# One of eight PSUM evictions per group given to VectorE in the edge-expansion stage of a graph layer

## The reference, cut to what matters

```
support = layernorm(x) @ W1
msgs = vals[:, None] * support[cols]            # one row of 256 per edge, 212500 edges
agg  = segment_sum(msgs, rows, num_segments=12500) + support
out  = relu(batchnorm(agg));  out = spmm_plus_eye(rows, cols, vals, out @ W2)
x = x + out
x = x + moe(layernorm(x))                       # 8 experts, top 2, D = 256
```

## Time and profile before

| | |
|---|---|
| median of three runs | 4718.69 us |
| span of the profiled execution | 4733.0 us |
| first stage in it | about 140 to 1235 us |
| busy over the span | TensorE 82%, VectorE 74%, ScalarE 64%, POOL 59% |
| busy in 140 to 1240 us | TensorE 83%, VectorE 82%, ScalarE 85%, POOL 68% |
| granted TensorE clock in 140 to 1240 us | 0.97 of full speed |

### The profile page before, as it was taken

How to read it: one execution, slowest core, us unless ns; L and a number is a source line. 1 busy time by engine, 2 the same in 40 slices (tenths; PEclk the granted TensorE clock), 3 DMA queues, 4 the chain that set the end, 5 groups by cost and what they waited for, 6 DMA issues and landing times.

```text
span 4733.0 us, 85423 instructions
## 1 busy us (share of the span) xinstructions
PE 3862.0 (82%) x26914; PEld 3364.9 (71%) x26914; DVE 3483.6 (74%) x9932; ACT 3025.5 (64%) x6515; POOL 2790.4 (59%) x2961
## 2 busy tenths in 40 slices
PE   1688888888798998855788888888888888888888
PEld 1687877788677777734677777777777777777777
DVE  8888888888688888855666777666777667667666
ACT  3688888888777787743555565555555545555555
POOL 0467676767565665456666666666666656666441
PEclk9999999999899999966899898899988989998999
DMA  8788888888888999663333333333333333333221
GB/s 238 278 304 306 309 309 305 311 305 285 286 297 302 302 317 304 235 194 108 91 103 98 97 104 96 97 101 96 99 100 97 97 96 102 97 98 103 77 76 28
DMA packets 308803, 858.01 MB, mean 181 GB/s; under 512 B 47937, under 2 KB 133018, under 8 KB 305852
## 3 DMA queue, kind: packets, MB, share of 16 engines
q0 software_dynamic: 140032, 442.58, 28.5%
q1 hardware_dynamic: 166148, 396.53, 26.5%
q10 hardware_dynamic: 2172, 13.35, 0.8%
HBM read 545.71 MB, written 306.56 MB: 180 GB/s over the span
## 4 chain that ended last, share of the span: by engine, by line
PE 49%; DVE 20%; ACT 10%; issue 10%; another core or an unknown queue 5%; DMA 4%; POOL 1%; SPq 0%; ACTq 0%; DVEq 0%; POOLq 0%
PE ps L1713 11%; PE ps L1734 8%; PE ps L1456 4%; PE ps L1604 3%; PE ps L886 3%; DMA L<-msgd 3%; PE ps L844 2%; PE ps L855 2%; PE ps L1608 2%; DVE S L1402 2%; PE ps L887 2%; PE ps L1606 2%; PE ps L843 2%; ACT A L951 2%
## 5 line engine op out<-in xcount | busy, mean ns | idle before, releaser
L1532 POOL DMA_INDIRECT G<-h,tabT x1440 | 1421.0, 987 | 941.1 <-issue 372.0
L1813 ACT ACTIVATE ps<-ps,b1T 128x500 f32<-128x500 f32 (+1 forms) x432 | 267.1, 618 | 827.1 <-PE ps L1713 551.9
L951 ACT ACTIVATE A<-ps,A 128x256 f32<-128x256 f32 x1728 | 690.4, 513 | 101.8 <-PE ps L887 98.0
L1002 POOL DMA_INDIRECT msgd<-A,tabT x432 | 542.9, 1257 | 307.5 <-ACT A L951 205.8
L1585 ACT ACTIVATE gH<-G,tabT 128x256 fp32r<-128x256 f32 x960 | 449.2, 499 | 222.1 <-remote 95.5
L1564 DVE SCALAR_TENSOR_TENSOR gL<-G,tabT,gH 128x256 fp32r<-128x256 f32 x960 | 459.1, 478 | 138.9 <-ACT gH L1585 90.9
L886 PE MATMUL ps<-winH,DT 128*128 128x256 f32 x1728 | 474.9, 306 | 67.5 <-issue 40.0
L1980 DVE SCALAR_TENSOR_TENSOR X<-ps,X 125x256 f32<-125x256 f32 x800 | 348.0, 478 | 235.1 <-remote 134.2
L1552 DVE TENSOR_SCALAR s<-iota,tabT 128x125 fp32r<-128x125 f32 x1600 | 518.9, 338 | 0.0
L1606 PE MATMUL ps<-gH,s 128*125 128x256 f32 x1067 | 357.8, 336 | 154.0 <-DVE s L1552 66.1
L887 PE MATMUL ps<-winL,DT 128*128 128x256 f32 x1728 | 437.7, 285 | 0.5 <-issue 0.5
(11 more groups left out here) (339 smaller groups left out, 11143.4 us busy)
## 6 DMA issues: line engine op xcount, KB each, us to landing
L<-msgd SPq DMA_DIRECT2D x400, 520.0 KB, 5.7
A<-sbd SPq DMA_DIRECT2D x54, 861.0 KB
msgd<-A SPq DMA_DIRECT2D x100, 325.0 KB
G<-h,tabT POOLq DMA_INDIRECT x1440
winR<-h SPq DMA_DIRECT2D x108, 128.0 KB
A<-in_x SPq DMA_DIRECT2D x10, 1120.0 KB
h<-A ACTq DMA_DIRECT2D x10, 1120.0 KB
acc<-h SPq DMA_DIRECT2D x10, 1120.0 KB
```

What stands on the lines that cost most here:

```text
L951: e.activation(M[:, n, 0:F], psum[4 + v % 4][:, (n % 2) * F:(n % 2 + 1) * F], ACT.Identity, scale=M[:, n, F + 2:F + 3]).then_inc(evc, 1)
L1002: e.indirect_dma_start(msgd, bass.IndirectOffsetOnAxis(ap=idxI[g % 4][:, t:t + 1], axis=0), msg[g % 3][:, t * 4 * RW:(t + 1) * 4 * RW], No ...
L1532: e.indirect_dma_start(B.G[c % GRL], None, of, bass.IndirectOffsetOnAxis(ap=tab3[:, m, 0:1].bitcast(I32), axis=0)).then_inc(gatl[c % GRL], 16)
```

## The change

Of the eight pairs of a group, number 3 (DVP) is evicted by VectorE with one instruction for both tiles: a tensor_tensor whose first stream is the whole bank in PSUM (128x512) and whose second stream is the two weights, each repeated 256 times. ScalarE evicts the other seven pairs as before. VectorE's eviction of group g stands right behind dve_place(g+1) and waits until pair 8g + 3 is expanded. A counter of its own, evd, tells TensorE, POOL and the verdict that the pair is out.

```diff
+DVP = 3
+def act_evicted(v):
+    return 2 * (v + 1 - (v + 1 + 8 - DVP - 1) // 8)

+        def dve_evict(e, g):
+
+            v = 8 * g + DVP
+            M = msg[g % 3].rearrange("p (t k) -> p t k", k=RW)[:, 2 * DVP:2 * DVP + 2, :]
+            e.wait_ge(recd, 3 * (g + 1))
+            e.wait_ge(exq, v + 1)
+            e.tensor_tensor(M[:, :, 0:F], psum[4 + v % 4][:, :].rearrange("p (n f) -> p n f", n=2),
+                            M[:, :, F + 2:F + 3].broadcast_to([P, 2, F]), ALU.mult).then_inc(evd, 1)

# dve_messages
                 if g + 1 < G2:
                     dve_place(e, own, g + 1)
+                dve_evict(e, g)
                 if g % 2 == 0:

# pe_expand
                 if v >= 4:
-                    e.wait_ge(evc, 2 * (v - 3))
+                    if (v - 4) % 8 == DVP:
+                        e.wait_ge(evd, (v - 4) // 8 + 1)
+                    else:
+                        e.wait_ge(evc, act_evicted(v - 4))

# act_messages, scale
                     v = 8 * g + n // 2
+                    if n // 2 == DVP:
+                        continue

# pool_messages
-                    e.wait_ge(evc, 16 * g + 4 * t + 4)
+                    e.wait_ge(evc, act_evicted(8 * g + 2 * t + 1))
+                    if t == DVP // 2:
+                        e.wait_ge(evd, g + 1)

# dve_verdict
-            e.wait_ge(evc, 16 * G2)
+            e.wait_ge(evc, act_evicted(8 * G2 - 1))
+            e.wait_ge(evd, G2)
```

More of the change, by code:

```diff
@@ L388, in build @@
         nrr, trir, bcd, rhsr, selr, slt, spr, prm = (sem(n) for n in ("nrr", "trir", "bcd", "rhsr", "selr", "slt", "spr", "prm"))
-        recd, dlc, dlt, dtc, bcr, dtd, exq, evc, wsl = (sem(n) for n in ("recd", "dlc", "dlt", "dtc", "bcr", "dtd", "exq", "evc", "wsl"))
+        recd, dlc, dlt, dtc, bcr, dtd, exq, evc, evd, wsl = (sem(n) for n in ("recd", "dlc", "dlt", "dtc", "bcr", "dtd", "exq", "evc", "evd", "wsl"))
         msgz, fillm = sem("msgz"), sem("fillm")
```

## The result

The changed kernel takes 5093.17 us (median of four runs, 5088.2 to 5100.23) against 4716.91 us for the kernel before: 376 us more, a ratio of 1.078 (95% interval 1.0762 to 1.0798). Slower was forecast, but the time lies 23 us above the range and 122 us above the predicted one. The profiled execution has a span of 5089.6 us.

A forecast was written before the change was run, and what follows sets the result against it. VectorE was taken as nearest its limit in the first stage, with the loop closing through it. Holds of 307 us, less 124 of old waits, plus 69 for the clock, gave 252 us on 4719: 4971 us, range 4865 to 5070.

The forecast's parts named there:

- ScalarE's saving is worth nothing: First stage: two evictions fewer a group, 78 us in all, only lengthen ScalarE's waits for TensorE; costed at nothing.
- The eviction at 0.69 us: VectorE's new double eviction, 108 times, takes 0.69 us each, bounds 0.19 and 1.00.
- The hold at full clock, 2.18 us: VectorE waits behind dve_place for TensorE's placing and expansion, 2.18 us; with start and eviction 2.92 us, 105 times, 307 us.
- VectorE's old waits are given back, 124 us: VectorE's waits before L738 and L721, 113.6 and 10.2 us, vanish because it gets there later.
- The net of 183 us: First stage: holds of 307 us less 124 us of old waits, before any clock term.
- TensorE is held at L831 and the select: VectorE's late L709 and L730 make TensorE stand there, about 1.2 us at L831; absorbed by its 5 to 6 us spare.
- The clock, 69 us: First stage: clock falls to 0.775, half speed 45% of the time, adding 1.47 us to that share of 105 holds.
- VectorE's other instructions at their old lengths: First stage: the sum has no term for VectorE's untouched instructions getting longer or shorter.
- nearly every restart: Rival: after nearly every hold TensorE restarts at 1.2 GHz, adding 154 us to 183, 5056 us; chance 0.14.
- the clock's bound: Limits of the first stage's clock term: none or all of the holds at half speed, 0 and 154 us.

The follow-up runs named there:

- e8: Changed kernel with 32 unused matmuls filling TensorE's pause and POOL's split moved behind the first scatter: 201 us over the kernel before, ratio 1.0421.
- b0: The kernel before, unaltered, profiled again on another chip: 4725.04 us, evictions' length 1049.4 us.
- e4: Changed kernel with 32 unused matmuls a group filling TensorE's pause before its wait for dve_place: 256 us over the kernel before, ratio 1.0613.
- e6: Changed kernel with POOL's split moved from ahead of the group's four scatters to behind the first: 240 us over the kernel before, ratio 1.0561.
- e10: Changed kernel with POOL's split behind the first scatter and dve_place's second instruction done three times: 380 us over the kernel before, ratio 1.0906.

## Why the prediction was wrong

The mechanism was right: a hold behind dve_place in every group, ended by pair 3's expansion; and slower was given 0.93. Two steps of the sum failed. The term for the clock was too small, 69 us, and the lengths of VectorE's other instructions were left as they were, without a reason. Together they measure 179 us of evictions' length where the sum had 69. The terms, by the prediction's steps:

- *ScalarE's saving is worth nothing.* Right. Its wait for L906 rose by 76 us, and with pair 1, where the same work is taken from it, the time did not move.
- *The eviction at 0.69 us.* Right: 692 ns.
- *The hold at full clock, 2.18 us.* Nearly: 2.42 us of idle time with the pause filled, against 2.22 in the sum. It also came in the last three groups, 108 times in all.
- *VectorE's old waits are given back, 124 us.* Right but for 8 us: 113.6 and 10.2 us became 7.5 and 0.
- *The net of 183 us.* Shown as a kernel (e8): 183 us of evictions' length (190 against b0), +201 us of time, with full clock and the placing instructions at their old lengths. The exact number is in part luck, as said there.
- *TensorE is held at L831 and the select.* Right: 29.8 us before L847 and 30.5 before L859 (L831 and L843 before), and VectorE hardly waits for TensorE behind the hold (7.5 us before L744).
- *The clock, 69 us.* The first failed step. It took the mean clock of a stretch, 0.775, for the share of holds that start at half speed, 0.45. The stage's mean clock was higher than that, 0.83, and still about (3.61 - 2.42)/1.47 = 0.8 of the hold's clock penalty was paid: the half speed falls upon the matmuls right behind the pause, and those are the ones in the hold. Filling the pause gives back 129 us (e4), or 44 us when the split is moved as well (e8 against e6). Nor could the clock be read off TensorE's busy share in other stages: it is 75% in the changed kernel's stage and in e6's (1089.12 of 1461 us, 991.95 of 1324) at clocks of 0.83 and 0.92, and 76% in e10's at 0.80.
- *VectorE's other instructions at their old lengths.* The second failed step, a term put at nothing. In the new rhythm POOL's split runs beside dve_place, and L768, L772, L775 and L798 grew by some 65 us in all (10, 34, 9 and 12), while L729, L713 and L725 lost some 28. Moving the split gives back 135 us of evictions' length (e6), or 50 us when the pause is filled as well (e8 against e4).

The two are not independent. Evictions' length in us, each cell from another chip (the same kernel repeats within 1 us for the changed one and 7 us for the one before):

| | restarts as they come | pause filled |
|---|---|---|
| split beside dve_place | 1418.7 | 1289.3 |
| split later | 1283.4 | 1239.5 |

Alone, the clock costs 44 us and the interference 50; together 179, so 85 us come only when both are there. The 44 is somewhat low, since the fillers in e8 also make TensorE late at times. The padded kernel shows the link without POOL: what lengthens dve_place lengthens TensorE's pause, and more of the placing runs at half clock, so that the hold grows from 2.99 to 3.67 us. That the longer pause is what lowers the clock is inferred from this; no kernel had the pause changed alone and unfilled. The prediction named "nearly every restart" as a rival at 5056 us and gave it 0.14; about 0.8 of them is what came, with the interference on top. The range's upper end stood at 5070, built from the clock's bound, but with no bound for instructions that the change does not touch.

The prediction held a figure of the Trainium skill against its clock term: the time lost in a clock ramp is under 1% of a typical kernel's span (TensorE: Matmul & The Clock Gate, The HAM clock gate). That figure stands beside the one warm-up of a kernel, and it does not carry over to a stage in which TensorE restarts in every group: filling the pause brought 131 us, 2.8% of the time, in e4, and 44 us of evictions' length, about 1%, with the split moved as well (e8 against e6).

## What to carry to other kernels

Before an engine is given a wait, ask which work has to run between its last output and what it waits for; if its own output is what releases that work, the engine stands idle for all of that work, while the same instruction on an item that was finished earlier (pair 1) cost nothing here. A wait that ends with the matmuls right behind a pause of TensorE is to be priced with these matmuls at 1.2 GHz, not at a stretch's mean clock: here about 0.8 of that price was paid, at a mean clock of 0.83. And a change in rhythm moves which instructions of VectorE and POOL run at the same time: bound the lengths of the untouched ones too.

## What was not expected of the hardware

- Useless matmuls in TensorE's pause made a kernel 2.8% faster (4615.11 to 4483.61 us, on two chips on which the kernel before takes 4226 and 4228 us).
- 0.6 us a group added to VectorE cost 1.3 us a group, while TensorE's clock in the stage went from 0.92 to 0.80.
- The kernel before took 4222 to 4228 us on three chips and 4717 and 4722 us on two others. The changed kernel's two profiles show where: its first stage ends at 1597 us in both, and behind it lie 5089.6 - 1597 = 3492 us on one chip and 4608.9 - 1598 = 3011 us on the other. The cause was not studied.
